# A PE sort for the first routed pass, an accumulating last gather, and a shorter preparation of attention

## What is computed

```python
x = x + 0.5 * ffn(layernorm(x))          # "first" feed-forward
x = x + attn(layernorm(x))               # 16 heads of 16, causal, adds its own input once more
x = x + 0.5 * ffn(layernorm(x))          # "second" feed-forward
# ffn: 2 experts; each token uses the one with the larger logit, scaled by its probability
sel  = argmax(softmax(x @ gate_w.T)); top_w = probs[sel]
h    = silu(x @ w_gate[sel].T) * (x @ w_up[sel].T)      # FF = 1024
out  = (h @ w_down[sel].T) * top_w
# attn: q, k, v = rms_norm(x) @ Wq, Wk, Wv;  softmax(causal(q k^T) / 16) v @ Wo + x
```

## Time and profile before

| What | Value |
|---|---|
| Median of 3 executions | 1255.71 us |
| The profiled execution, its own time | 1255.95 us |
| Its span, from the first to the last instruction | 1254.2 us |
| Instructions | 39207 |
| TensorE busy | 1078.9 us, 86% |
| VectorE, ScalarE, GpSimd busy | 860.2, 744.7, 571.8 us |
| Mean granted clock of TensorE | 0.963 |

### The profile page before, as it was taken

How to read it: one execution, slowest core, us unless ns; L and a number is a source line. 1 busy time by engine, 2 the same in 40 slices (tenths; PEclk the granted TensorE clock), 3 DMA queues, 4 the chain that set the end, 5 groups by cost and what they waited for, 6 DMA issues and landing times. The chain is left out here.

```text
span 1254.2 us, 39207 instructions
## 1 busy us (share of the span) xinstructions
PE 1078.9 (86%) x14566; PEld 933.9 (74%) x14566; DVE 860.2 (69%) x1784; ACT 744.7 (59%) x1285; POOL 571.8 (46%) x693
## 2 busy tenths in 40 slices
PE   0677889986979989989998799998999999989894
PEld 0666778775868877778777678877777888778774
DVE  6643646785767886767787867888677797775421
ACT  3532525674757866666676667775766676776321
POOL 3146544344352344645354545334573255655443
PEclk9889889997989999989999899999999999999998
DMA  8203251212211122122223041112321112211211
GB/s 316 84 24 90 66 94 45 78 45 81 59 53 48 32 63 75 47 64 64 80 60 94 25 112 53 41 33 70 81 81 36 53 33 73 84 50 49 53 44 47
DMA packets 110670, 83.99 MB, mean 67 GB/s; under 512 B 59616, under 2 KB 104416, under 8 KB 110496
## 3 DMA queue, kind: packets, MB, share of 16 engines
q1 hardware_dynamic: 93408, 54.22, 15.7%
q0 software_dynamic: 6144, 17.31, 4.3%
q10 hardware_dynamic: 10944, 9.97, 2.5%
HBM read 37.26 MB, written 34.23 MB: 57 GB/s over the span
## 5 line engine op out<-in xcount | busy, mean ns | idle before, releaser
L676 POOL TENSOR_TENSOR h_lo<-hid,h_hi 128x256 bf16<-128x256 f32 x304 | 217.7, 737 | 480.9 <-ACT h_hi L743 479.9
L814 ACT ACTIVATE area<-ps_w,s_scale 128x512 f32<-128x512 f32 x320 | 219.4, 686 | 218.0 <-PE ps_w L1216 170.1
L1135 PE MATMUL ps_g<-x_t,w 128*128 128x128 f16 x1096 | 209.8, 226 | 15.5 <-issue 9.2
L1029 DVE TENSOR_TENSOR area<-area 128x512 f16<-128x512 f32 x256 | 206.6, 807 | 18.9 <-ACT area L815 15.4
L815 ACT ACTIVATE area<-ps_w,s_scale 128x512 f16<-128x512 f32 x320 | 218.0, 681 | 0.0
L1137 PE MATMUL ps_g<-x_t,w 128*128 128x128 f16 x1096 | 209.9, 226 | 2.0 <-issue 1.8
L1136 PE MATMUL ps_g<-x_t,w 128*128 128x128 f16 x1096 | 209.1, 225 | 1.8 <-issue 1.8
L1135 PE MATMUL ps_u<-x_t,w 128*128 128x128 f16 x1096 | 205.6, 222 | 2.9 <-issue 2.7
L1137 PE MATMUL ps_u<-x_t,w 128*128 128x128 f16 x1096 | 205.8, 222 | 1.7 <-issue 1.5
L1136 PE MATMUL ps_u<-x_t,w 128*128 128x128 f16 x1096 | 204.5, 221 | 1.8 <-issue 1.8
L1154 PE MATMUL ps_y<-wd,h_hi 128*128 (+1 forms) x608 | 169.1, 278 | 14.8 <-POOL h_lo L676 12.1
(11 more groups left out here) (160 smaller groups left out, 2806.8 us busy)
## 6 DMA issues: line engine op xcount, KB each, us to landing
y_sorted<-ys ACTq DMA_DIRECT2D x76, 128.0 KB
qk_scratch<-area SPq DMA_DIRECT2D x32, 256.0 KB
qt<-qk_scratch SPq DMA_DIRECT2D x128, 64.0 KB, 2.7
kt<-qk_scratch SPq DMA_DIRECT2D x128, 64.0 KB, 2.8
x_buf<-x SPq DMA_DIRECT2D x8, 512.0 KB, 4.3
out<-x_buf SPq DMA_DIRECT2D x8, 512.0 KB, 2.9
x_sorted<-zeros SPq DMA_DIRECT2D x18, 136.0 KB, 2.0
area<-w_down SPq DMA_DIRECT2D x4, 512.0 KB, 12.8
```

The lines of the kernel that those rows point to most:

```text
L676: pool.tensor_tensor(h_lo[:, u % 2, c], hid[:, u % 2, c], h_hi[:, u % 2, c], ALU.subtract).then_inc(h_lo_done, 1)
L814: act.activation(p_f32[:, f % 3], ps[:], ACT.Exp, scale=s_scale[:])
L1029: dve.tensor_tensor(p_lo[:, f % 4], p_f32[:, f % 3], p_hi[:, f % 4], ALU.subtract).then_inc(lo_done, 1)
L1135: pe.matmul(cols, w_hi, x_hi, start=kb == 0 and f == 0, stop=False, skip_group_check=True)
```

## The change

**The first pass is sorted on TensorE.** POOL writes a ramp 0 to 639 in float16 (`places`). `l_pos` of item 0 makes four 128x640 matrices `perm` (one where a token's place equals the column). A new stage `x_perm` multiplies the split rows `xs` by them: 16 matmuls of 512 columns to four banks and 16 of 128 columns to `ps_y`; ACT copies the four banks to `x_t`, DVE the fifth in `w_scale` 0. The transposing DMA of pass 0 is gone; scatter and load of the coefficient stay. The zeroing of scratch 0 moves behind the weights on SP, 9 blocks at once instead of 5 and later 4. On DVE the first four maxima go ahead of `l_dlogit`, the other four behind `l_pos` and `l_coef`; each now waits for itself (`link`). Unit 0's gate and up wait for each weight piece by itself.

**The last gather is accumulated and stored by quarters.** For item 15 the four indirect DMAs add to `x_buf` directly; each has a semaphore, SP stores each quarter as it lands, and POOL's `x_update` is gone there.

**The plan.** Attention starts at point 97 instead of 115, parts take 21.3 instead of 21. Batches 0 and 2 (`AT_ONCE`) have their norm, transposes, projections and first `qk_in` in about half the points before their first part. `OUT_AT` is 2.5 points later.

```diff
-PART_AT = 115
-PART_POINTS = 21
+PART_AT = 97
+PART_POINTS = 21.3
...
+NORM0_AT = [-20, -19.8, -19.4, -18.4, -17, -16]
+RESIDUAL0_AT = -13
+PROJ0_AT = [-15.2, -13.7, -12.2, -10.7, -9.2, -7.7]
+QK_IN0_AT = -12
+AT_ONCE = (0, 2)
...
-OUT_AT = [122, 123.5, 125.5, 127.5]
+OUT_AT = [124.5, 126, 128, 130]
...
+PERM_AT = -55.7
+MAX_AT = [-59.56, -59.54, -59.52, -59.5, -55.5, -55.4, -55.3, -55.2, -51.2, -51, -46.8, -46.6]
...
-            at = min(at, part_at(GROUPS * b, NORM_AT[0]) - 1)
+            at = min(at, part_at(GROUPS * b, NORM_AT[0] if b not in AT_ONCE else NORM0_AT[0]) - 0.5)
...
+    put(PERM_AT, "x_perm")
...
-        for where, stage in zip(NORM_AT, norm):
+        for where, stage in zip(NORM_AT if b not in AT_ONCE else NORM0_AT, norm):
             put(part_at(first, where), *stage)
-        put(part_at(first, RESIDUAL_AT), "residual", b)
+        put(part_at(first, RESIDUAL_AT if b not in AT_ONCE else RESIDUAL0_AT), "residual", b)
         for m in range(NP):
-            put(part_at(first, PROJ_AT[m]), "proj", b, m)
-            put(part_at(first, PROJ_AT[m] + STORE_LAG), "qk_store", b, m)
+            at = part_at(first, (PROJ_AT if b not in AT_ONCE else PROJ0_AT)[m])
+            put(at, "proj", b, m)
+            put(at + STORE_LAG, "qk_store", b, m)
...
-        put(part_at(p, QK_IN_AT[p % GROUPS]), "qk_in", p)
+        put(part_at(p, QK_IN0_AT if p in (0, 2 * GROUPS) else QK_IN_AT[p % GROUPS]), "qk_in", p)
...
+        perm = x_t[1][:, 0:T * P * SLOTS[0]].rearrange("p (i t) -> p i t", i=T)
+        places_i = yt[0][:].rearrange("p i d -> p (i d)")[:, 0:P * SLOTS[0]].bitcast(I32)
+        places = yt[1][:].rearrange("p i d -> p (i d)")[:, 0:P * SLOTS[0] // 2].bitcast(F16)
+        perm_banks = [ps_g, ps_u, ps_v[0], ps_v[1]]
...
-                if w == GU_PIECES // 2 - 1:
+                if w == GU_PIECES + DOWN_PIECES - 1:
+                    sp.dma_start(x_of(1)[:], batch_view(x, 1)).then_inc(x_in[1], 16)
                     sp.wait_ge(zero_ready, 1)
-                    zero(0, range(SLOTS[0]))
-                elif w == GU_PIECES + DOWN_PIECES - 1:
-                    sp.dma_start(x_of(1)[:], batch_view(x, 1)).then_inc(x_in[1], 16)
+                    zero(0, range(MAX_SLOTS))
...
+                    if n == 1:
+                        sp.wait_ge(x_perm, 5)
+                    if n:
+                        sp.dma_start_transpose(x_t_of(n), x_sorted[n % 2][0:P * SLOTS[n], 0:D].bitcast(F16)).then_inc(xt_loaded, 16)
...
-                        zero(0, range(SLOTS[0], MAX_SLOTS))
...
+                    if k == len(ITEMS) - 1:
+                        for i in range(T):
+                            sp.wait_ge(last_in[i], 16)
+                            sp.dma_start(out[b, i * P:(i + 1) * P], x_of(b)[:, i, :]).then_inc(x_out[b], 16)
+                        continue
...
+            link(pool.iota(places_i, pattern=[[1, P * SLOTS[0]]], base=0, channel_multiplier=0))
+            link(pool.tensor_copy(places, places_i))
...
-                    if p == 0:
-                        pool.wait_ge(zeroed[0], 16 * SLOTS[0])
-                    elif p < 3:
-                        pool.wait_ge(zeroed[p % 2], 16 * MAX_SLOTS)
-                    if p >= 2:
-                        pool.wait_ge(xt_loaded, 16 * (p - 1))
+                    if p < 2:
+                        pool.wait_ge(zeroed[p], 16 * MAX_SLOTS)
+                    elif p > 2:
+                        pool.wait_ge(xt_loaded, 16 * (p - 2))
...
+                    if n == len(ITEMS) - 1:
+
+                        b = ITEMS[n][3]
+                        for i in range(T):
+                            pool.indirect_dma_start(
+                                x_of(b)[:, i, :], None, y_sorted[p % 2][0:P * SLOTS[p], :],
+                                bass.IndirectOffsetOnAxis(ap=place[n % ROUTES][:, i:i + 1], axis=0), compute_op=ALU.add
+                            ).then_inc(last_in[i], 16)
+                        continue
...
+                elif what == "x_perm":
+                    for c in range(2 * KB):
+                        act.wait_ge(x_perm, c + 1)
+                        act.activation(x_t_of(0)[:, c, 0:S], perm_banks[c][:], ACT.Copy).then_inc(x_t_copied, 1)
...
-                    ins = dve.tensor_reduce(w_max[:, w:w + 1], stage[w], AX.X, ALU.max, apply_absolute_value=True)
-                    if w == GU_PIECES - 1:
-                        link(ins)
-                        dve.tensor_reduce(w_max1[:, 0:1], w_max[:, 0:GU_PIECES], AX.X, ALU.max).then_inc(w_max_done, 1)
+                    link(dve.tensor_reduce(w_max[:, w:w + 1], stage[w], AX.X, ALU.max, apply_absolute_value=True))
...
+                    if k == 0:
+                        dve.wait_ge(x_perm, 5)
+                        dve.tensor_copy(x_t_of(0)[:, :, S:], ps_y[:].rearrange("p (c t) -> p c t", c=2 * KB)
+                                        ).then_inc(x_t_last, 1)
...
+                    if n == 0:
+                        link(dve.tensor_tensor(place_f[:], high_place[:], ps[:, 0:T], ALU.add))
+                        for i in range(T):
+                            dve.tensor_scalar(perm[:, i, :], places, place_f[:, i:i + 1], None,
+                                              ALU.is_equal).then_inc(perm_ready, 1)
...
+                elif what == "x_perm":
+                    pe.wait_ge(l_hi, 1)
+                    for c in range(2 * KB):
+                        part, cols = c // KB, slice(c % KB * P, (c % KB + 1) * P)
+                        if c == KB:
+                            pe.wait_ge(l_lo, 1)
+                        for i in range(T):
+                            if c == 0:
+                                pe.wait_ge(perm_ready, i + 1)
+                            ins = pe.matmul(perm_banks[c][:], xs[:, i, part, cols], perm[:, i, 0:S], start=i == 0,
+                                            stop=i == T - 1, skip_group_check=True)
+                        ins.then_inc(x_perm, 1)
+                    for c in range(2 * KB):
+                        part, cols = c // KB, slice(c % KB * P, (c % KB + 1) * P)
+                        for i in range(T):
+                            ins = pe.matmul(ps_y[:, c * P:(c + 1) * P], xs[:, i, part, cols], perm[:, i, S:],
+                                            start=c == 0 and i == 0, stop=c == 2 * KB - 1 and i == T - 1,
+                                            skip_group_check=True)
+                    ins.then_inc(x_perm, 1)
...
+                    if u == 0:
+                        pe.wait_ge(w_ready, KB * kind + kb + 1)
                     if kb == 0:
-                        if u == 0:
-                            pe.wait_ge(w_ready, KB * (kind + 1))
-                        elif u == 2:
+                        if u == 2:
                             pe.wait_ge(w_ready, GU_PIECES)
                         if s == 0 and q == 0 and what == "gate":
-                            pe.wait_ge(xt_loaded, 16 * (n + 1))
+                            if n == 0:
+                                pe.wait_ge(x_t_copied, 2 * KB)
+                            else:
+                                pe.wait_ge(xt_loaded, 16 * n)
...
+                        if u == 0:
+                            pe.wait_ge(x_t_last, 1)
```

More of the change, by code:

```diff
@@ L104 @@
 GU_PIECES, DOWN_PIECES = 8, 4
+SUM_PIECES = list(range(GU_PIECES, GU_PIECES + DOWN_PIECES))
 PIECES = GU_PIECES + DOWN_PIECES + KB
@@ L565, in _ @@
             for b in range(B):
[L566 removed]
+                sp.wait_ge(x_out[b], 16 * (T if b == ITEMS[-1][3] else 1))
         @block.gpsimd
@@ L626, in _ @@
                             xs_rows[:, i, :], None).then_inc(scattered, 16)
-                elif what == "x_update":
+                elif what == "x_update" and st[1] < len(ITEMS) - 1:
                     n = st[1]
@@ L687, in _ @@
                 what, ps = st[0], bank_of.get(st)
-                if what == "w_max" and st[1] >= GU_PIECES:
+                if what == "w_max" and st[1] in SUM_PIECES:
                     w = st[1]
                     act.wait_ge(w_in[w], 16)
-                    if w > GU_PIECES:
-                        act.wait_ge(w_sum_done, w - GU_PIECES)
+                    if w != SUM_PIECES[0]:
+                        act.wait_ge(w_sum_done, SUM_PIECES.index(w))
                     act.activation(flat(hid[:]), stage[w], ACT.Abs,
```

18 lines of the change are left out of this document (11 added, 7 removed).

## The result

| | before | changed |
|---|---|---|
| median of 7 runs each, us | 1256.56 (1254.37 to 1260.17) | 1267.18 (1262.06 to 1272.96) |
| ratio | | 1.0086, 95% interval 1.0061 to 1.0112 |
| profiled execution, us | 1255.95 | 1272.96 (span 1271.2) |

The changed kernel is slower by 0.9%, some 11 us, where 10 us less were forecast. Two later sets of runs of it gave 1.0108 (1.0083 to 1.0132) and 1.0062 (1.0035 to 1.0089). The profiled execution is its slowest of the seven, so its trace shows some 6 us more than the median. Lines are those of each run's own kernel: L1169, L1060, L1197 and L1214 of before are L1242, L1109, L1270 and L1287 in the changed kernel and L1228, L1095, L1256 and L1273 in e8, h1 and h2.

A forecast was written before the change was run, and what follows sets the result against it. TensorE, busy 86% of the span, was taken as the bound, its matmuls a floor. 1255.95 - 1.1 - 2.8 - 5.5 + 1.6 - 2.5 = 1245.65, against the median 1245.4 us; range 1235 to 1257.

The forecast's parts named there:

- A: Start: sorting on TensorE removes the wait for the transposing DMA; tanh 0 at 37.1, -1.1 us (-2.3 to +1.0).
- B: Batch 0 prepared later and faster, attention 18 points earlier: waits added, x_t wait and low clock removed, -2.8 us (-8 to +4).
- C: Batch 2: statistics move later, so the 5.6 us stall and its low clock go; -5.5 us (-9 to 0).
- rival 2: Batch 2: its stall only moves, statistics or transposes wait again; 1250.9 us, or 1252 with low clock; chance 0.13.
- rival 3: More than priced: two stalls behind ScalarE and POOL go too, by another phase of p_lo; 1238 us, chance 0.14.
- D: Attention ends 7.1 points earlier, so 1.2 more units run with 1.4 us of holes each: +1.6 us (0 to +3).
- E: Last gather adds in the DMA and stores by quarters, POOL's 2.34 us add goes: -2.5 us (-3.3 to -0.3).
- The rest: Parts of 21.3 points instead of 21 only shift score fills against units: priced at 0, with 6 either way.
- the slower rival: TensorE's in-order queue at the squeezed preparations makes projections wait for their banks: 15.6 us more, 1261 us, chance 0.07.
- faster: Sign of the whole change: faster than before by more than about 0.2%, 2.5 us; chance given as 0.86.

The follow-up runs named there:

- e8: Changed kernel with attention back at 115, parts of 21 and the old last gather; squeezed preparations and later `OUT_AT` kept: ratio 1.0036 to before.
- h1: Changed kernel's sort with the old plan and old last gather, plus only batch 2 prepared in half the time: ratio 0.9994 to before.
- h2: Changed kernel with the old plan and old last gather, so the sort alone, run a second time: ratio 0.9954 to before.
- f3: Changed kernel's sort, attention at 115 prepared as before, old last gather, but parts of 21.3 and `OUT_AT` 2.5 points later: ratio 1.0297 to before.
- e2: Changed kernel with the old plan, keeping the sort and the last gather that adds: ratio 1.0010 to before.
- e1: Changed kernel with the old plan and old last gather, so the sort alone: ratio 0.9978 to before.
- e4: Whole changed kernel with parts of 21 points instead of 21.3: ratio 1.0206 to before.
- f4: Changed kernel with idle matmuls put into three of TensorE's waits: ratio 1.0064 to before.

## Why the prediction was wrong, point by point

**A, the start: right, a little small.** -1.1 us forecast, -1.8 measured: tanh 0 at 36.37 instead of 38.16. The rows that answer:

```profile
19.28 1.27 DVE L977 TENSOR_SCALAR x_t<-yt,place_f 128x640 f16<-128x640 f16 x4
...
28.88 4.26 ACT L737 ACTIVATE w<-qt,w_scale 128x1024 f16<-128x1024 f32 x4 [0.32 <-DVE g_scale L904]
...
36.37 0.67 ACT L778 ACTIVATE hid<-ps_g,g_scale 128x512 f32<-128x512 f32 x1
...
19.81 1.86 PE L1165 MATMUL ps_g<-x_t,xs_rows 128*128 128x512 f16 x4 [0.83 <-DVE x_t L977]
...
25.48 1.06 PE L1171 MATMUL ps_y<-x_t,xs_rows 128*128 128x128 f16 x16
```

TensorE's sort ends at 26.5, as forecast, but by two misses that cancel: it starts at 19.81, not 18.5, and takes 6.7 us, not 8.0, because its last eight matmuls of 512 columns take 0.29 us each and only the first eight 0.42. The scale comes at 28.9 (29.3 forecast). A compare takes 0.32 us (1.27/4), not the 0.5 I took. The Trainium skill (VectorE: DVE Perf Modes, Mode 4x_2P) had given 0.32 by its rule for 16-bit tensors; the trace agrees. That the sort alone is worth 3 to 6 us by the end is more than its 1.8 us at the start. Where the rest comes from is open.

**B, batch 0: the waits below their range, the gain not there.** The two named waits came out at 4.69 and 1.67 us, 6.4 for the forecast 7 to 9. The wait for x_t of 3.67 us is gone; what TensorE idles nearby is 0.87 us inside the gate of an earlier unit, for which the profile shows no cause:

```profile
125.94 1.09 PE L1242 MATMUL ps_w<-ident,area 128*128 128x128 f32 x4 [4.69 <-ACT area L809]
...
130.82 0.76 PE L1109 MATMUL ps_w<-xt_hi,wa_hi 128*128 128x512 f32 x1 [1.67 <-issue]
...
173.32 0.22 PE L1208 MATMUL ps_g<-x_t,w 128*128 128x128 f16 x1 [0.87 <-issue]
```

Yet between 60 and 200 us idle time and low clock together grew by 1.2 and 1.8 us in two traces and 6.6 in one, where -2.8 was forecast. What stands there now is a new wait for x_t near 98 us (2.1 to 2.3 us in these traces; it is 1.5 to 2.4 us in e8, h2 and f3 too, which have the sort and not the new lead) and low clock that only moved, from 174 us to 157 or 161.

**C, batch 2: the mis-sized term.** -5.5 us forecast. VectorE's statistics no longer wait for x_update, as the earlier trace rows had it, though x_update, which I had taken to hardly move, came 4.1 us later than before; the transposes wait instead (POOL, DVE, PE):

```profile
355.78 2.35 POOL L658 TENSOR_TENSOR x_buf<-yt,x_buf 128x1024 f32<-128x1024 f32 x1
...
360.37 1.39 DVE L1006 BATCH_NORM_STATS2 bn<-x_buf 128x6 f32<-128x256 f32 x4
...
367.10 1.09 PE L1242 MATMUL ps_w<-ident,area 128*128 128x128 f32 x4 [3.78 <-ACT area L809]
```

3.78 us where I had counted 2.5, and 6.8 us at the lower clock behind it as before, where I had let all of that go. This is rival 2, "the stall only moves": between 345 and 385 us idle time and half-clock are 10.8 and 10.3 us before and 10.7, 10.4 and 9.8 after. h1 against h2 puts the step by itself at +5 us with the rest as before, not -5.5. The 7.2 us that 200 to 420 us did give came from elsewhere: 4.2 us between 280 and 325 us, which is part of rival 3, and 2.8 ahead of it. TensorE's longest waits there, for ScalarE's exp and for POOL's p_lo, were 5.77 and 3.42 us in the earlier trace rows and are 2.79 and 1.87 here, and low clock behind them stays (17.0 and 10.2 us before, 10.2 to 13.7 after):

```profile
296.50 0.39 PE L1270 MATMUL ps_w<-kt,qt 65*128 65x512 f16 x1 [2.79 <-ACT area L856]
...
302.05 0.41 PE L1307 MATMUL ps_v<-v_parts,area 128*128 128x33 f16 x8 [1.87 <-POOL area L717]
```

**D, attention's end: no size to be seen.** The last pair of exp starts 114.2 us ahead of the end of the span, 108.1 before: 6 us, where 9 were forecast. f3 shows that the other direction is steep, 37 us for an attention that ends later, though not all of it at the end.

**E, the last gather: mis-sized.** ScalarE's last tanh, GpSimd's first and last issue, SP's last store:

```profile
1251.51 0.69 ACT L778 ACTIVATE hid<-ps_v,g_scale 128x512 f32<-128x512 f32 x1 [0.35 <-PE ps_v L1208]
...
1259.57 1.63 POOL L679 DMA_INDIRECT x_buf<-y_sorted,place  x1 [3.88 <-issue]
...
1265.21 1.54 POOL L679 DMA_INDIRECT x_buf<-y_sorted,place  x1 [0.30 <-issue]
...
1269.04 0.33 SPq L555 DMA_DIRECT2D out<-x_buf  x1
```

From the last tanh to the end of the span 19.7 us, 20.45 before: 0.8 gained, 2.5 forecast. An issue of the gather that adds takes 1.53 to 1.63 us, a plain one 0.95 to 1.04, so the fourth leaves 2.4 us later than it would; that eats the add of 2.34 us. From the start of the fourth issue to the add, or to the last store, 3.8 us pass instead of 2.8; 0.6 of this difference is the issue's, so the landing costs about the 0.4 us that I had taken. I had looked for the price in the landing alone and left the four issues out. e2 against e1 shows no gain either (1.0010 and 0.9978).

**"The rest": the step that failed.** "Only shifts score fills against units", priced at 0 with 6 either way. It is +18.4 us between 640 and 1000 us. I had followed the two places where the diff is thick and two neighbours, and had taken the other 900 us as left alone, though PART_AT and PART_POINTS move all 320 score fills against every routing, gather and scatter, whose points stay. The 18 points of lead stood in that stretch at the same nothing: e4, with parts of 21, loses 63.1 us there (38.6 and 37.5 before). By the planner's points, batch 5's preparation (483 to 505, before 495 to 517) came to lie on the routing of 480 to 504 points, in the step of +5.9 us, and batch 7's (653 on, before 663 on) behind the x_updates of 646 and 651, in the step of +5.1. Which meetings cost is open: e8, with its parts where they lay before, loses as much between 700 and 760 us as the changed kernel (17.0 us, against 14.2 to 18.2) and gets it back beside it. A term that moves every part of a long stretch against fixed work has a range of its own, and f3 and e4 show how wide it is here: +2 to +3%. The mechanism of the slower rival, a queue of TensorE at the squeezed preparations, was not it: batch 0's projections wait 1.67 us at most and batch 2's 0.4. Its sign was right, with 0.07 far too little. (The chances of "faster" add up to 0.87, not 0.86.)

## What to carry to other kernels

A constant that sets the phase of two interleaved streams is no small term, even where its own arithmetic gives zero. Price it over the whole length, and test it alone: parts 1.4% longer (with `OUT_AT` 2.5 points later) cost 3% of the time here. A lead with the old preparations and the old parts was never run here; it is the run to start with. A stall that a shift removes in one place tells nothing of the ones it makes where the other stream's fixed work lies. And compare TensorE's clock with its idle time, but don't take the clock for the cause: with the same idle time the changed kernel had 10 to 12 us more booked to the clock per run, and taking most of that away (f4) won nothing.

## What the runs showed of the hardware

- The same sum of idle time (159 us in both traces of one chip) went with 100 or 139 us at the lower clock. Raising the clock behind three waits with other matmuls (f4) gave no time.
- VectorE's TENSOR_SCALAR of 128x4 at 872.74 took 1.97 us, where the median of its 16 is 0.17. It ended at 874.71, when GpSimd's operation of 872.38 ended (874.68). By the Trainium skill (SBUF — State Buffer, SBUF: two separate sides) the two engines share a pair of ports under a lock that is held for a whole instruction, and one of them waits if VectorE's operation needs the pair. This row agrees: a tiny operation as long as the neighbour's rest.
- An indirect DMA that adds costs GpSimd 1.53 to 1.63 us per issue, a plain one 0.95 to 1.04.
